# An attention and expert layer in three stages on one core: 128-column filter bands, spread fillers, and a solve moved into the last stage

## What is computed

```
v = silu(causal_dwconv(x @ Wv, conv_v_w))                # 256 channels, 384 tokens, 32 images
fir_long = causal_dwconv(v, fir_long_w)                  # 63 taps, each channel its own
A = tril(einsum(kb, k), -1);  T = inv(I + A)             # per chunk of 32 tokens
u = T @ v_beta;  w = T @ k_beta                          # then the scan over chunks
delta, S = scan(step, S, (q, k, u, w))
gate_in = [x, mean and std of fir_short, fir_long, delta, v]
o = mix of fir_short, fir_long, delta, v by softmax(mlp(gate_in)); h = h + norm(o) @ Wo
h = h + experts(layernorm(h))
```

## Time and profile before

| | us |
|---|---|
| median of 3 runs | 2378.38 (2372.26 to 2381.79) |
| the profiled execution's own time | 2393.8 |
| its span in the profile | 2392.1 |
| first stage, to the barrier | about 655 |
| second stage, first to last matmul | 656.0 to 811.9 |
| third stage, from its first matmul | 817.7 |
| one step of the third stage, in the middle | 47.5 |

### The profile page before, as it was taken

The page is one execution under the profiler, slowest core; times in us unless marked ns, Lnnn a source line. Parts: engine busy times, 40 slices in busy tenths (PEclk is TensorE's granted clock), DMA queues, the critical chain, the costliest instruction groups (busy, mean ns, idle before and its releaser), DMA issues.

```text
span 2392.1 us, 53303 instructions
## 1 busy us (share of the span) xinstructions
PE 2251.9 (94%) x20796; PEld 1635.1 (68%) x20796; DVE 1852.8 (77%) x5111; ACT 1290.8 (54%) x2632; POOL 555.5 (23%) x413
## 2 busy tenths in 40 slices
PE   5999999999799779999999999999999999999997
PEld 4666666666587666777677767776776677767765
DVE  4999999999868367677778777777777667767765
ACT  4888888888624334544454455445544544454452
POOL 1444444444400011121112111111111121112111
PEclk9999999999958879999999999999999999999999
DMA  3776777777778912233224222322233224222300
GB/s 98 231 245 229 229 241 245 236 238 236 247 241 314 378 60 71 71 108 96 78 70 139 91 77 71 125 81 74 70 132 105 71 70 133 77 71 76 125 21 21
DMA packets 224297, 334.44 MB, mean 140 GB/s; under 512 B 113870, under 2 KB 190766, under 8 KB 215342
## 3 DMA queue, kind: packets, MB, share of 16 engines
q1 hardware_dynamic: 219726, 309.01, 39.1%
q10 hardware_dynamic: 2304, 12.58, 1.3%
q0 software_dynamic: 2016, 9.44, 1.0%
HBM read 191.66 MB, written 164.23 MB: 149 GB/s over the span
## 4 chain that ended last, share of the span: by engine, by line
PE 49%; DVE 7%; ACT 6%; issue 4%; POOL 0%; DVEq 0%
PE bank L1662 7%; PE bank L1672 7%; PE bank L1595 6%; PE bank L1475 4%; PE bank L1555 4%; PE bank L1632 4%; PE bank L1571 2%; PE bank L1507 2%; PE bank L1543 2%; ACT L1808 2%; ACT L1803 2%; DVE v_all L2111 1%; PE bank L1503 1%; PE bank L1485 1%; DVE DL L2019 1%
## 5 line engine op out<-in xcount | busy, mean ns | idle before, releaser
L2111 DVE SCALAR_TENSOR_TENSOR v_all<-bank,we,v_all 128x256 f32<-128x256 f32 x576 | 264.9, 476 | 219.3 <-PE bank L1672 214.3
L739 DVE SCALAR_TENSOR_TENSOR Y<-bank,convw,Y 128x383 f32<-128x383 f32 (+2 forms) x576 | 330.6, 602 | 3.2 <-ACT Y L627 2.9
L1672 PE MATMUL bank<-w2e,HE 128*128 128x256 f32 x1152 | 327.9, 395 | 2.4 <-DVE v_all L2111 2.3
L1662 PE MATMUL bank<-v_all,w1e 128*128 128x384 f32 x768 | 289.6, 500 | 2.4 <-ACT HE L1808 2.3
L445 PE MATMUL bank<-pb,wqkv 128*128 128x384 f32 x768 | 282.4, 491 | 1.8 <-DVE Y L739 1.8
L1672 PEld LDWEIGHTS bank<-w2e,HE 128*128 128x128 f32 x1152 | 198.0, 191 | 55.3 <-issue 19.3
L1808 ACT ACTIVATE HE<-bank 128x384 f32<-128x384 f32 x192 | 94.1, 490 | 248.9 <-PE bank L1662 248.2
L1595 PE MATMUL bank<-v_all,w1g 128*128 128x384 f32 x512 | 193.4, 500 | 2.0
L1662 PEld LDWEIGHTS bank<-v_all,w1e 128*128 128x128 f32 x768 | 134.5, 191 | 75.9 <-issue 19.8
L445 PEld LDWEIGHTS bank<-pb,wqkv 128*128 128x128 f32 x768 | 132.1, 191 | 61.1 <-DVE Y L739 8.3
L1786 ACT ACTIVATE first_stage<-bank 32x384 f32<-32x384 f32 (+1 forms) x192 | 92.2, 480 | 135.7 <-PE bank L1583 119.2
(11 more groups left out here) (217 smaller groups left out, 5199.1 us busy)
## 6 DMA issues: line engine op xcount, KB each, us to landing
packa<-pa SPq DMA_DIRECT2D x32, 1932.0 KB, 6.2
v_all<-packa SPq DMA_DIRECT2D x32, 1932.0 KB, 8.1
packb<-pb SPq DMA_DIRECT2D x32, 768.0 KB, 6.1
v_all<-packb SPq DMA_DIRECT2D x32, 768.0 KB, 10.8
toeplitz<-taps SPq DMA_DIRECT2D x128, 190.0 KB, 5.3
toep<-toeplitz SPq DMA_DIRECT2D x32, 760.0 KB, 7.6
packb<-fsk SPq DMA_DIRECT2D x32, 384.0 KB, 2.7
first_stage<-fl SPq DMA_DIRECT2D x32, 384.0 KB, 8.7
```

The costliest lines, as they stand in the source:

```text
L739: dve.scalar_tensor_tensor(out=Y[:, j, lag:T], in0=proj_bank[j][:, 0:T - lag], scalar=convw[:, j, CK - 1 - lag:CK - lag], in1=Y[:, j, lag: ...
L1662: mm = pe.matmul(bank[6][:, 0:T], w1e[:, a, k, :], YT[s][:, a, :], start=(a == 0), stop=(a == HALF - 1))
L1672: pe.matmul(expert_bank(b), HE[k % 2][:, b * P:(b + 1) * P], w2e[:, k, :], start=True, stop=True)\
L2111: dve.scalar_tensor_tensor(out=HA[s][:, b, :], in0=expert_bank(b), scalar=we[s][:, b, k:k + 1], in1=HA[s][:, b, :], op0=ALU.mult, op1=ALU. ...
```

## The change

1. **Bands.** In rows 0 to 63 of a matrix only columns 0 to 125 differ from zero, in rows 64 to 127 only columns 64 to 189. `toeplitz` now holds 128 columns per row and channel, from column 0 or from column 64 on. TW is 192. A group is loaded by two DMAs of 64 rows each, into columns 0:128 and 64:192 of `toep`, in pieces of 512 bytes (8 per row) in place of one piece of 6080 bytes per row. VectorE clears columns 0:64 of rows 64 to 127 once. The second set of matmuls reads rows 64 to 127 alone and has 64 columns of weights.
2. **Fillers.** 3 before the wait for the first load and 4 behind it; 1 ahead of each odd group; 2 ahead of groups 8, 16 and 24. That is 29 where there were 14.
3. **Solve.** The second stage solves sets 0 and 1 alone. The third solves sets 2 and 3 in steps 0 to 19, three columns in each: one in `solve_first`, behind `transpose_diagonal`, and two in `solve_others`, where `solve_columns` stood. GpSimd loads set 3 right behind the store of set 1.
4. **Store.** The last four stores of `fl` go from ScalarE at the end of the second stage to SyncE at the start of the third.
5. **VectorE's order in the third stage.** `delta_out(n, 0)` goes ahead of `routing_weights`, `remainder(n, 1)` ahead of `weigh`, `remainder(n, 2)` ahead of two `add_expert`. The six `input_stats` of image 0 go to near the end of step 0.

```diff
-TW = P + FL - 1
+BAND = P
+TW = DH + BAND
-SPLIT = 20
+SOLVE_PASSES = (SC - 2) // 3
...
-                        sp.dma_start(dram["toeplitz"][p], dram["taps"][:, bass.ds(P - 1 - p, TW)]).then_inc(expanded, 16)
+                        sp.dma_start(dram["toeplitz"][p], dram["taps"][:, bass.ds(P - 1 - p + p // DH * DH, BAND)])\
+                            .then_inc(expanded, 16)
...
-                    sp.dma_start(toep[it % NT][:, :, :], dram["toeplitz"][:, it * CG:(it + 1) * CG, :])\
-                        .then_inc(toep_loaded[it % NT].sem, 16)
+                    for k in range(P // DH):
+                        rows = slice(k * DH, (k + 1) * DH)
+                        sp.dma_start(toep[it % NT][rows, :, k * DH:k * DH + BAND],
+                                     dram["toeplitz"][rows, it * CG:(it + 1) * CG, :]).then_inc(toep_loaded[it % NT].sem, 16)
...
-                dense(5)
+                dense(3)
                 for i in range(0, groups // NT):
                     for s in range(NT):
                         it = i * NT + s
-                        if it and it % GI == 0:
-                            dense(3)
+                        if it:
+                            dense(it % 2 if it % GI else 2)
                         pe.wait_ge(*toep_loaded[s].now(i))
+                        if it == 0:
+                            pe.wait_ge(tail["toep_cleared"], NT)
+                            dense(4)
...
-                                mm = pe.matmul(acc[0:TW - P, o + NB:o + BLK * NB], toep[s][:, ch, P:],
-                                               v_all[:, it * CG + ch, 0:(BLK - 1) * NB],
+                                mm = pe.matmul(acc[0:TW - P, o + NB:o + BLK * NB], toep[s][DH:P, ch, P:],
+                                               v_all[DH:P, it * CG + ch, 0:(BLK - 1) * NB],
...
-                act.wait_ge(*fl_copied.now(NH * GI - 1))
-                for q in range(FQ):
-                    store(NH - 1, q)
...
-                load(3, 0, 2 * SOLVE_STEPS + 9)
-                load(3, 1, 2 * SOLVE_STEPS + 17)
-                load(3, 2, 2 * SOLVE_STEPS + 25)
+                for part in range(SG):
+                    load(3, part)
...
+                for s in range(NT):
+                    dve.memset(toep[s][DH:P, :, 0:DH], 0.0).then_inc(tail["toep_cleared"], 1)
...
-                solve["begin"](dve, 2)
-                for j in range(1, SPLIT):
-                    solve["column"](dve, 2, j)
...
+                sp.wait_ge(*tail["fl_copied"].now(D // 8 - 1))
+                for q in range(FQ):
+                    store_filtered(NH - 1, q)
                 sp.wait_ge(fl_stored[2], 16 * FQ)
...
+                def solve_first(n):
+                    if n < 2 * SOLVE_PASSES:
+                        g, turn = 2 + n // SOLVE_PASSES, n % SOLVE_PASSES
+                        if turn == 0:
+                            solve_begin(dve, g)
+                        solve_column(dve, g, 1 + 3 * turn)
+
+                def solve_others(n):
+                    if n < 2 * SOLVE_PASSES:
+                        g, turn = 2 + n // SOLVE_PASSES, n % SOLVE_PASSES
+                        solve_column(dve, g, 2 + 3 * turn)
+                        solve_column(dve, g, 3 + 3 * turn)
```

More of the change, by code:

```diff
@@ L101, in audio_tower @@
             "taps": nc.dram_tensor("taps", [D, 512], F32, kind="Internal").ap(),
-            "toeplitz": nc.dram_tensor("toeplitz", [P, D, TW], F32, kind="Internal").ap(),
+            "toeplitz": nc.dram_tensor("toeplitz", [P, D, BAND], F32, kind="Internal").ap(),
         }
@@ L942, in kept_semaphores @@
                   late_stored=sem("late_stored"), fl_stored=[sem(f"fl_stored{g}") for g in range(NH)],
-                  toep_loaded=[Signal(sem(f"toep_loaded{s}"), 16, primed=0) for s in range(NT)],
+                  toep_cleared=sem("toep_cleared"),
+                  toep_loaded=[Signal(sem(f"toep_loaded{s}"), 16 * P // DH, primed=0) for s in range(NT)],
                   fl_ready=Signal(sem("fl_ready"), 2, primed=0), fl_copied=Signal(sem("fl_copied"), 2, primed=0))
@@ L1448, in step, with store_filtered @@
                         load_u(sp, n + 2, n % 2)
+                def store_filtered(g, q):
+                    part = NB * BLK * DH // FQ
+                    sp.dma_start(dram["fl"][g][:, q * part:(q + 1) * part], stage[g][:, q * part:(q + 1) * part])\
+                        .then_inc(fl_stored[g], 16)
+                sp.wait_ge(*tail["fl_copied"].now(D // 8 - 1))
+                for q in range(FQ):
+                    store_filtered(NH - 1, q)
                 sp.wait_ge(fl_stored[2], 16 * FQ)
@@ L2113, in add_expert @@
                         .then_inc(acc_done.sem, 1)
-                def columns_of(n):
-                    if n < 6:
-                        at = SPLIT + min(3 * n, 5 + n)
-                        return 2, at, at + (3 if n < 2 else 2 if n == 2 else 1)
-                    at = 1 + 2 * (n - 6)
-                    return 3, at, at + 2
-                def solve_columns(n):
-                    if n > 20:
-                        return
-                    g, first, last = columns_of(n)
-                    if first == 1:
-                        solve_begin(dve, g)
-                    for j in range(first, last):
-                        solve_column(dve, g, j)
+                def solve_first(n):
[9 more added lines that the diff above has]
+                        solve_column(dve, g, 3 + 3 * turn)
                 def step(i):
@@ L2174, in step @@
                         transpose_diagonal(n, n % 2, 0, 0, n // 2).then_inc(tdiag_ready.sem, 1)
+                        solve_first(n)
                     if 0 <= f < NB:
                         add_expert(f, 4, 0)
-                    if 0 <= n < NB:
+                    if 0 < n < NB:
                         input_stats(n, 0)
@@ L2192, in step @@
                         add_expert(f, 4, 2)
+                    if 0 < n < NB:
+                        input_stats(n, 5)
                     if 0 <= n < NB:
-                        input_stats(n, 5)
-                        solve_columns(n)
+                        solve_others(n)
                     if 0 <= f < NB:
@@ L2209, in step @@
                         gate_weights(it)
+                    if 0 <= n < NB:
+                        delta_out(n, n % 2, 0)
                     if 0 <= e < NB:
                         routing_weights(e, e % 2)
+                    if 0 <= n < NB:
+                        remainder(n, 1)
                     if 0 <= it < NB:
                         weigh(it, it % 2, 2)
-                    if 0 <= n < NB:
-                        delta_out(n, n % 2, 0)
-                        remainder(n, 1)
                     if 0 <= f < NB:
@@ L2234, in step @@
                         mix_add(it, it % 2, 4, tb[:, :].rearrange("p (m d) -> p m d", d=DH))
+                    if 0 <= n < NB:
+                        remainder(n, 2)
                     if 0 <= e < NB:
@@ L2238, in step @@
                     if 0 <= n < NB:
-                        remainder(n, 2)
                         delta_out(n, n % 2, 1)
@@ L2246, in step @@
                         delta_out(n, n % 2, 2)
+                    if n == 0:
+                        for j in range(NM // 2):
+                            input_stats(n, j)
                     if 0 <= e < NB:
```

## The result

| kernel | median, us | ratio to before (95% interval) |
|---|---|---|
| before | 2377.05 (9 executions, 2372.26 to 2383.14) | |
| changed | 2397.62 (9 executions, 2388.25 to 2413.31) | 1.0089 (1.0066 to 1.0112) |

The change made the kernel 0.9% slower. The prediction was 2338 us (2321 to 2363), faster by 1.7%, with 0.04 for slower. The profiled execution of the changed kernel took 2394.6 us, that of before 2393.8: the two traces are equally long although the medians differ by 20 us. Both facts need an explanation.

A forecast was written before the change was run, and what follows sets the result against it. It took VectorE to bound the first stage and TensorE the second (a sixth slow clock) and third. Terms of -15.2, -3.9, +1.5 and -22.9 sum to -40.5 us; applied to the median 2378.4, that gave 2338 us (2321 to 2363).

The forecast's parts named there:

- Second stage, DMA: Second-stage loads: a group takes 1.75 us instead of 1.87, 127 us of DMA work in 141, with 3 us of waits.
- Rival 1: Second stage: small pieces make loads the bound at 2.50 us a group; 2348 us, 2367 with one clock fall; chance 0.18.
- Second stage, TensorE: Second stage: fillers keep TensorE at full clock, so it takes 140.6 us against 155.8, a gain of 15.2 us.
- GpSimd's loads at 0: Second stage's end: GpSimd issues three loads some 20 us ahead of TensorE's end, at no cost.
- in a place I can't see: Low end of the range: some 11 us more, since the runs shown differ from the profiled execution by 15.4 us.
- moving the sum over by 15.4: Whole kernel: the same -40.5 us applied to the median 2378.4 instead of the profiled 2393.8, giving 2338 us.
- The barrier, -3.9: Between second and third stage: with ScalarE's last stores moved, TensorE waits about 2 us instead of 5.9.
- Step 0, +1.5: Third stage's first step: a VectorE wait goes (0.4 us gained), but moved statistics delay image 1's masks by 1.9.
- Third stage, -22.9: Every third-stage step: TensorE's waits for DL and R both end whole, 0.74 us in each of 31 steps.
- rival 2: Third stage: each of the two removed waits is replaced by another, from a later `add_expert` or column; 2361 us; chance 0.13.
- Columns, 0: Third stage, steps 0 to 19: the added solve columns fit into VectorE's idle time, at no cost.

The follow-up runs named there:

- Kernel 2: The changed kernel with one load per group over all 128 partitions, still in 512-byte pieces, all to columns 0 to 127: 2375.90 us, 0.9988 of before.
- kernel 3: The changed kernel with full rows of 6080 bytes, each group still loaded by two DMAs of 64 partitions: 2398.98 us, 1.0085 of before.
- kernel 5: The changed kernel with the loads of partitions 64 to 127 issued from ScalarE's queue, the others from SyncE's: 2378.71 us, 0.9998 of before.
- kernel 7: The kernel before with only the change's moves of DL and R in VectorE's third-stage step: 2372.89 us, 0.9994 of before.
- kernel 9: The kernel before with only the moves of solve groups, last filter stores and first batch's statistics: 2376.10 us, 0.9990 of before.
- kernel 10: kernel 1 with the fillers of before (five at the start, three at each eighth group): 2369.05 us, 0.9961 of before.
- kernels 13 and 14: Kernel 11 with the first statistics back in their old place: 2362.19 us; the same plus `add_expert(f, 5, 2)` ahead of `weigh`: 2363.75 us.
- Kernel 11: kernel 1 with the four small routing operations ahead of the gate weights in VectorE's third-stage step: 2362.82 us, 0.9919 of before.
- kernel 1: The changed kernel with the loads of before, whole rows in one load of 128 partitions per group: 2368.35 us, 0.9959 of before.
- kernel 4: The changed kernel with full rows and two loads per group, each of four channels over all 128 partitions: 2374.49 us, 0.9982 of before.
- kernel 6: The kernel before with only the change's bands (two loads of 64 partitions, 512-byte pieces): 2412.61 us, 1.0137 of before.

## Why the prediction was wrong

**The DMA term failed.** "Second stage, DMA" priced a group at 1.75 us between ends of 1.60 and 2.50, and all three came from pieces of a given size. The change's loads differ in a second way that I didn't price: each covers half the partitions. Kernel 2 (same pieces, all partitions) is at 0.9988, kernel 3 (long rows, half the partitions) at 1.0085. In the change a stretch such as 704 to 708 moved 180 GB/s at a share of 1.25; 524 KB take 2.9 us at that rate, above the upper end of my range and near the 3.7 us in which TensorE uses a group, with the stores and systems still to be carried. The whole stage says the same: 164 us at a share of 1.02 are 167 us of DMA work where I had 127. With 131 - 32 x 1.87 = 71 us for everything else, as before, that leaves an estimated 3.0 us a group for my 1.75. The Trainium skill, SBUF — State Buffer, Door 1: The DMA port swizzle, has this: partitions 0 to 63 reach 8 of the 16 ports, and 196 GB/s were measured there where all 128 gave 328. The trace agrees, with 180 GB/s in the change from 704 to 708 and 185 from 688 to 692. The same page, Can I just issue two DMAs to hit both halves?, says that issuing from several engines does not help; kernel 5 contradicts that in time (19 of 29 us back) and supports it in rate early on (204 GB/s), and the measurement decides.

**Rival 1 was the case, for another reason.** It had "the small pieces make the loads the bound" and 2367 with one fall of the clock. The loads did become the bound and the clock fell twice, behind waits of 2.5 and 3.7 us. But its price, 2.50 us a group, was too low (an estimated 3.0), and it had no way to end slower than before.

**"Second stage, TensorE", -15.2, was right in size and set against the wrong base.** With full rows the stage took 140 us, against 140.6 predicted; four fillers raised the clock, and it held. The base of 155.8 is an execution with 25.5 us of half clock. 15 of 95 executions are as long as that; the median is 17 us shorter. With full clock TensorE is done at 785 and does not end the stage: GpSimd's loads do, at 798.5 (kernel 7) and 795.0 (kernel 9), with VectorE's columns just ahead in kernel 7; and where neither does, a late load holds TensorE itself until 794.5 (kernel 10). I had put GpSimd's loads at 0, which holds only while TensorE ends later than they land. So in the median this term is worth nothing. The sentence that some 15.4 us lay "in a place I can't see" was the warning: if the common execution is like that of kernel 7, they lay in the very term I was about to collect, and moving the sum over by 15.4 counted them twice. No trace of the kernel before itself shows that.

**The barrier, -3.9**, measured -4.6 (1.3 for 5.9) in the profiled pair. It is right there; where GpSimd ends the stage, as in kernel 7, moving ScalarE's stores gains nothing.

**Step 0, +1.5**: 75.4 us from the third stage's start to the first mark against 72.5, so +2.9. The clock differs between the executions, and kernels 13 and 14 did not separate it.

**Third stage, -22.9, gave -5.5** (31 x 0.18). "Both waits should end whole" came true, but I counted their whole length as gain and did not ask what TensorE would wait for next. Behind the wait for DL stood the first R, `remainder(n, 1)`, which the prediction never priced. In the change it moved past `weigh` alone and stays behind the four routing operations, whose length under GpSimd's products was not priced either. So TensorE now waits 0.44 us for it where it had waited 0.43 for DL. The sign was there: one operation on 18 elements at 1.07 us where its neighbours take 0.17. Kernel 11 shows the mechanism: with the routing operations ahead of the products they take 0.18 each, no R is waited for, and a step is 0.34 us shorter still. The Trainium skill, SBUF — State Buffer, Who interferes with whom, says that a VectorE instruction with two SBUF inputs contends with a GpSimd instruction that reads SBUF, and that the loser blocks. The trace agrees: the two TENSOR_TENSOR took 1.24 and 1.00, the TENSOR_REDUCE between them 0.17. So rival 2 (each wait is replaced by another) was the case in kind. One of the new waits is for an `add_expert`, as it said; the larger is for the first R, which it did not name, and 0.18 of the 0.74 us stayed as gain.

**Columns, 0**: right. TensorE has no wait for them, and kernel 9 is no slower for them.

**The sum in the median.** Bands +29.3 (change less kernel 1); the order -4.4 (kernel 7); the moves -1.0 (kernel 9); the fillers -0.7 (kernel 1 less kernel 10). That is +23, against 2397.6 - 2377 = +20.6; the remainder is within the intervals of the single runs. Each of the last three terms is by itself no larger than its interval.

## What to carry to other kernels

Let every load cover all 128 partitions. A third fewer bytes in two loads of 64 partitions cost 29 us here, and one load of full rows was the fastest of the six ways tried. Before pricing a term on one profiled execution, compare its time and clock with those of the others; where they differ by more than the effect you look for, find out where, since the term may be that difference. Before naming what ends a stage, look at the end-of-block row of every engine: here it was GpSimd, which the windows show as nearly idle. When a wait is removed, look for the next thing that the waiting engine needs. When an operation is moved, look at which engine runs beside its new neighbours: a 0.17 us operation can take 1.2.

## What the runs showed of the hardware

- From 656 to 790 us, all traffic together, two loads of 64 partitions per group went with 244 GB/s at a share of 1.05 (512-byte pieces, the change) and 276 at 1.01 (6080-byte pieces, kernel 3); one load of 128 partitions with 273 at 0.86 (512-byte pieces, kernel 2) and 337 at 0.91 (6080-byte pieces, kernel 1); two loads of 128 partitions with 328 at 0.90 (kernel 4).
- 512-byte pieces into SBUF over all partitions went with 305 GB/s at a share of 0.94 (kernel 2, 700 to 730, all traffic), which is an estimated 1.6 us for 524 KB: the 768-byte row was the right neighbour.
- GpSimd's end-of-block DRAIN lasted until some 0.6 us behind the landing of its last load: 798.5 for 797.8 in kernel 7, 795.0 for 794.4 in kernel 9.
- How the clock fared at the start of the second stage went with the wait for the first load, with five fillers ahead of it. It was at half for tens of us where that wait was 2.0 to 2.8 us (the kernel before, twice, and kernel 6) and at 0.99 to 1.00 where it was 0.7 to 0.9 (kernels 7, 9 and 10). In the last three the second stage's fillers began at 657.4 to 659.1 us, in the others at 655.6 to 656.0, so the load had longer to land. With four fillers behind the wait the clock was full after them each time.
